# Last layer of a two-layer kernel: squares turned by TensorE, taps' end and mixed sum ahead of the last down product

## The chip, the cores and the metric

The kernel runs on one core of a Trainium2 chip. The metric is the device time of one execution in microseconds (us). The engines are TensorE (PE, with its weight loads PEld), VectorE (DVE), ScalarE (ACT), GpSimd (POOL) and SyncE (SP), which issues the DMAs.

## What is computed

Two layers over 8 sequences of 512 tokens with 128 channels. The first layer is attention times a mixture of experts; the second, which the change is in, is a gated recurrent block times a tanh feed-forward:

```python
def _L1_attn_ref(x, ...):
    h = rmsnorm(x, norm1_w)
    local = causal_depthwise_conv(h, conv_w)          # 7 taps
    decay = jnp.clip(jax.nn.sigmoid(h @ Wdecay + bdecay), 0.05, 0.95)
    gate = jax.nn.sigmoid(h @ Wgate + bgate)
    updates = gate * h
    cumdecay = jnp.exp(jnp.cumsum(jnp.log(decay), axis=1))
    weighted_updates = updates / jnp.maximum(cumdecay_shifted, 1e-07)
    state = jnp.cumsum(weighted_updates, axis=1) * cumdecay * state_scale
    mem = (h @ Wk) @ M.T @ Wmem * mem_scale
    mixed = x + jnp.concatenate([local, state, mem], axis=-1) @ Wc + bc
    h2 = rmsnorm(mixed, norm2_w)
    return mixed + jax.nn.silu(h2 @ Wg) * (h2 @ Wup) @ Wdown
...
x = x + s * g     # s from above, g = silu(tanh(xn @ weight @ aux_weight1 @ aux_weight2 + bias))
```

`rmsnorm` divides by the root of the mean square over the channels. The change concerns how `h2` gets this mean square, and when `mixed` of the next sequence is made.

## The kernel before

Every engine has a program written by hand, and semaphores tie them together; nothing but the written order and the waits sets when an instruction runs. The last layer goes over the eight sequences in steps b = 0 to 7, each with tiles of 128 channels by 512 tokens. While step b does the feed-forward of sequence b, it prepares sequence b+1 (turning, gates, decay, taps, state) and, through ACT and POOL, sequences b+2 to b+4 (normalising, gate of the first layer). Products go to eight banks of PSUM.

Names that the trace shows for tiles are those of the regions they lie in: `SPARE`, `WGE`, `W1E`, `W2E` hold the last layer's tiles. Lines of TensorE in a step: `d_conv_end` L975 and `d_state` L979 close bank 4 (taps, memory, state); `d_turn_scaled` L925, `d_ffn1` L985, `d_back` L1052 (turns the finished product of b-1 back), `d_squares` L992, `d_gates` L947 and L950, `d_roots` L998 (spreads the inverse roots), `d_turn` L933, `d_conv` L971, then four chunks c of `d_up` (L1012 gate, L1018 up) and four of `d_down` (L1044).

VectorE: `d_mixed` L1510, the radicands of sequence b+2 L1456 and L1459, `d_meansq` L1517 (mean square plus epsilon, `SSE`), `d_local` L1524 (taps 1 to 5, each adds to `LOC`), `d_add` L1572 (adds the product of b-1 to X), `d_h2_of` L1530, `d_decay` L1483, `d_cumulate` L1488, `d_floor` L1496, `d_gated` L1537 (four), `d_mean_scaled` L1476, `d_scan` L1503, `d_sum` L1568 (down product plus mixed), statistics L1445 and L1450.

GpSimd: `gate_out` L625 (waits for `d_sum`), `front` L594 and `add_x` L599 (sequence b+3), `rms` L629 (power -0.5 of `SSE`, waits for `d_meansq`, releases `d_roots`), `scales` L610, `update_gated` L615, `update` L620 (waits for the floor; the scan waits for it), `both` L634 (sequence b+4). ScalarE makes the squares of `mixed` (L1931) and copies, tanh and SiLU.

Before, the squares `SQR` are the weights of four matmuls with one column `MEAN` = 1/128, which gives the mean square of each token in one column of PSUM.

Of the kernel before, what the change touches and what calls it, by code (L numbers as in the profile page):

```python
# [26 lines left out]
P = 128  # L27
# [53 lines left out]
def build(nc, t, out):  # L81
    ctx = ExitStack()
    with ctx:
# [46 lines left out]
        MEAN = sb("MEAN", [P, 1])  # L130
# [107 lines left out]
        ST1 = small[:, 8 * TPS:14 * TPS].rearrange("p (i s) -> p i s", s=6)  # L238
        SSE, RS = (small[:, (16 + n) * TPS:(17 + n) * TPS] for n in range(2))
# [91 lines left out]
        done = sem("done")  # L331
# [14 lines left out]
        d_own = sem("d_own")  # L346
        d_xp, d_ve, d_vv, d_r1, d_hs, d_trh, d_da, d_gp, d_u1 = (
# [24 lines left out]
        def mixed(b):  # L372

            return MIXL if b == NSEQ - 1 else MIX

        def roots_bank(b):

            return 0 if b == NSEQ - 1 else 7

        def back_bank(b):  # L380

            return 1 if b == NSEQ - 2 else 5
# [122 lines left out]
        def _(pool):  # L505
# [143 lines left out]
            for b in range(NSEQ):  # L649
                if b == 0:  # L650
                    pool.wait_ge(d_sta, 1)
                    add_x(2)
                    both(3)
                elif b < NSEQ - 1:
                    gate_out(b - 1)
                    if b + 3 < NSEQ:
                        front(b + 3)
                        add_x(b + 3)
# [14 lines left out]
        def _(pe):  # L673
# [115 lines left out]
            def count():  # L789
# [4 lines left out]
                pe.wait_ge(prep, 3)  # L794
# [61 lines left out]
            pe.wait_ge(prep, 3)  # L856
# [61 lines left out]
            def d_turn_scaled(b):  # L918
                pe.wait_ge(d_hs, b + 1)
                if not (isinstance(b, int) and b == 0):  # L920
                    pe.wait_ge(d_ht, b)
                else:
                    pe.wait_ge(proj_free, 4 * NSEQ)
                for i in range(TPS):
# [62 lines left out]
            def d_squares(b):  # L987
                pe.wait_ge(d_sq, b + 1)
                if 0 < b < NSEQ - 1:
                    pe.wait_ge(d_s, b)  # L990
                for i in range(TPS):
                    mm = pe.matmul(B[roots_bank(b)][:, i:i + 1], SQR[:, i * P:(i + 1) * P], MEAN[:], start=True, stop=True)  # L992
                mm.then_inc(d_ss, 1)

            def d_roots(b):
                pe.wait_ge(d_rs, b + 1)
                for i in range(TPS):
                    mm = pe.transpose(B[roots_bank(b)][:, i * P:(i + 1) * P], RS[:, i:i + 1].broadcast_to([P, P]), ident)  # L998
# [49 lines left out]
            def d_back(b):  # L1048
                pe.wait_ge(d_of, b + 1)
                pe.wait_ge(d_sil, FC * b + FC)  # L1050
                for i in range(TPS):
                    mm = pe.transpose(B[back_bank(b)][:, i * P:(i + 1) * P], OF[:, i * P:(i + 1) * P], ident)  # L1052
                mm.then_inc(d_ot, 1)

            def d_step(b, first=False, last=False):

                if not first and not last:
                    d_conv_end(b)
                if not last:
# [20 lines left out]
                down = d_last_down if last else (lambda c: d_down(b, c))  # L1080
                down(0)
                d_up(b, 3)
                down(1)
# [13 lines left out]
            pe.wait_ge(prep, 3)  # L1097
# [7 lines left out]
            d_first_conv()  # L1105
            d_step(0, first=True)
# [8 lines left out]
        def _(dve):  # L1115
# [76 lines left out]
            def slots():  # L1192
# [5 lines left out]
                dve.wait_ge(prep, 3)  # L1198
# [365 lines left out]
            def d_sum(b):  # L1564
# [15 lines left out]
            def d_step(b, first=False, front=True):  # L1580
                if front and not first:
                    d_later_stats(b + 2)
                d_mixed(b)
# [22 lines left out]
                if b == NSEQ - 2:  # L1606
                    d_scan(b + 1)
                    d_gated(b, 3)
                    d_mixed(b + 1)
                else:  # L1610
                    d_gated(b, 3)
                    d_scan(b + 1)
                d_sum(b)

            def d_last_step(b):
# [458 lines left out]
```

## Time and profile before

| | us |
|---|---|
| median of 3 runs | 540.2 |
| lowest, highest | 539.59, 540.52 |
| profiled execution, its own time | 540.95 |
| its span, first to last instruction | 538.8 |
| PE busy | 519.0 (96%) |
| DVE busy | 397.5 (74%) |
| ACT busy | 314.6 (58%) |
| POOL busy | 223.7 (42%) |

The last layer fills the span from about 377 us on. A share of the whole span is an average over stages, so the stage is read in stretches: one for each step, from the end of the step's state product to the end of the next. The chain of waits goes backwards from the last instruction and tells which engine held the end. The timeline gives each instruction's start, its length and, in brackets, how long its engine had been idle and what ended that. [...]

### The profile page before, as it was taken

What the parts mean: (1) busy time and instruction counts of PE and PEld (TensorE: products, weight loads), DVE (VectorE), ACT (ScalarE), POOL (GpSimd) and SP (SyncE); (2) the same over time, 40 slices, a digit from 0 to 9 for tenths busy, and PEclk for the clock granted to TensorE, in tenths of its full rate; (3) what the DMA queues carried; (4) which work ended last, traced back from release to release, by engine and by line L of the source; (5) the groups of instructions that cost most, each with busy time, mean ns of one, the idle gap of its engine ahead of it and who ended that gap; (6) DMA issues with size and microseconds to landing.
All of it is one profiled execution on the core that took longest, in us unless ns stands there. A gap on an engine that the chain in (4) does not pass through costs nothing. (4 is left out here: it accounts for less than half of the span.)

```text
span 538.8 us, 12865 instructions
## 1 busy us (share of the span) xinstructions
PE 519.0 (96%) x3195; PEld 387.7 (72%) x3196; DVE 397.5 (74%) x1129; ACT 314.6 (58%) x832; POOL 223.7 (42%) x229
## 2 busy tenths in 40 slices
PE   9998898999998999999999999998999999999997
PEld 4755566666667999999999999986454545544544
DVE  6889669768885766777677767766788887788654
ACT  4733554555547656666666666667776576657512
POOL 4304453666640333333333333332667557623310
PEclk9999999999999999999999999999999999999999
DMA  9930743311126555555555555618300000000001
GB/s 283 395 115 28 229 152 127 99 60 66 40 45 52 155 131 156 132 155 138 152 137 152 141 151 141 151 47 225 94 0 21 0 20 21 19 0 21 19 7 33
DMA packets 84722, 55.37 MB, mean 103 GB/s; under 512 B 52928, under 2 KB 69600, under 8 KB 84432
## 3 DMA queue, kind: packets, MB, share of 16 engines
q1 hardware_dynamic: 80368, 46.04, 32.7%
q0 software_dynamic: 4320, 8.92, 4.6%
q8 instruction: 16, 0.26, 0.2%
q14 instruction: 18, 0.15, 0.1%
HBM read 37.62 MB, written 15.74 MB: 99 GB/s over the span
## 5 line engine op out<-in xcount | busy, mean ns | idle before, releaser
L1808 ACT ACTIVATE AR<-bank,BGT 128x128 f32<-128x128 f32 x284 | 81.2, 368 | 71.8 <-PE bank L870 69.6
L580 POOL DMA_INDIRECT rows_y<-YO,W1E x71 | 68.8, 969 | 126.5 <-DVE YO L1335 123.9
L541 POOL DMA_INDIRECT slots_x<-XR,SLOT x64 | 62.5, 977 | 52.6 <-DMA slots_x<-XR,SLOT 32.7
L1358 DVE SCALAR_TENSOR_TENSOR AR<-bank,B1T,AR 128x128 f32<-128x128 f32 x284 | 80.2, 344 | 5.1 <-ACT AR L1808 3.6
L870 PE MATMUL bank<-AR,WGE 128*128 128x128 f32 x568 | 76.7, 278 | 1.9 <-DVE AR L1341 1.7
L888 PE MATMUL bank<-W2E,AR 128*128 x568 | 75.1, 275 | 0.5 <-DVE AR L1358 0.5
L879 PE MATMUL bank<-AR,WGE 128*128 128x128 f32 x568 | 75.0, 275 | 0.0
L1724 ACT ACTIVATE AR<-bank,AR 128x512 f32<-128x512 f32 (+1 forms) x64 | 33.8, 528 | 64.2 <-DVE AR L1268 53.4
L870 PEld LDWEIGHTS bank<-AR,WGE 128*128 128x128 f32 x568 | 69.0, 192 | 2.9 <-issue 2.5
L888 PEld LDWEIGHTS bank<-W2E,AR 128*128 128x128 f32 x568 | 69.1, 192 | 0.7 <-issue 0.7
L879 PEld LDWEIGHTS bank<-AR,WGE 128*128 128x128 f32 x568 | 69.1, 192 | 0.0
L785 PE MATMUL bank<-AR 128*128 128x128 f32 x320 | 48.2, 281 | 2.8 <-ACT AR L1733 1.8
L1341 DVE STREAM_TRANSPOSE AR<-XG 128x128 f32<-128x128 f32 x71 | 22.1, 311 | 37.3 <-issue 22.3
L1268 DVE TENSOR_REDUCE AR<-bank 128x1 f32<-128x512 f32 (+1 forms) x64 | 31.1, 488 | 25.0 <-PE bank L752 19.1
L1801 ACT ACTIVATE WGE<-SPARE 128x512 f32 x71 | 45.4, 641 | 0.8 <-issue 0.5
L785 PEld LDWEIGHTS bank<-AR 128*128 128x128 f32 x320 | 40.7, 191 | 5.9 <-ACT AR L1733 4.6
L750 PE MATMUL bank<-AR 128*128 128x128 f32 (+3 forms) x128 | 45.0, 435 | 0.0
L766 PEld LDWEIGHTS bank<-CST,AR 128*128 128x128 f32 x160 | 18.9, 141 | 29.7 <-ACT AR L1724 15.9
L766 PE MATMUL bank<-CST,AR 128*128 128x128 f32 x160 | 29.1, 280 | 6.2 <-ACT AR L1724 5.8
L1948 ACT ACTIVATE W1E<-bank 128x512 f32<-128x512 f32 x32 | 19.0, 593 | 26.8 <-PE bank L1012 26.8
L1012 PE MATMUL bank<-WGE,WGT 128*128 128x512 f32 x64 | 32.7, 593 | 0.7 <-DVE X L1572 0.7
L1018 PE MATMUL bank<-WGE,WUP 128*128 128x512 f32 x64 | 32.7, 592 | 0.0
(214 smaller groups left out, 910.9 us busy)
## 6 DMA issues: line engine op xcount, KB each, us to landing
WGE<-in_wgu SPq DMA_DIRECT2D x71, 256.0 KB
XG<-slots_x SPq DMA_DIRECT2D x140, 32.0 KB
slots_x<-W1E SPq DMA_DIRECT2D x7, 585.0 KB, 10.1
X<-in_x SPq DMA_DIRECT2D x8, 256.0 KB, 5.1
SPARE<-in_wgu SPq DMA_DIRECT2D x1, 2048.0 KB
W2E<-in_w SPq DMA_DIRECT2D x1, 2048.0 KB
XR<-rows_y SPq DMA_DIRECT2D x8, 256.0 KB, 4.9
XNT<-rows_y SPq DMA_DIRECT2D x8, 256.0 KB, 5.4
```

The costliest lines, as they stand in the source:

```text
L541: pool.indirect_dma_start(out=slots_x, out_offset=bass.IndirectOffsetOnAxis(ap=SLOT[:, k, n:n + 1], axis=0), in_=XR[:, n, :], in_offset=No ...
L580: pool.indirect_dma_start(out=rows_y, out_offset=bass.IndirectOffsetOnAxis(ap=DST[:, j:j + 1], axis=0), in_=YO[q % 2][:], in_offset=None). ...
L750: pe.matmul(bank[:, 0:(i + 1) * P], QT[u][h][:, i * P:(i + 1) * P], QT[u][2][:, 0:(i + 1) * P], start=True, stop=False)
L766: mm = pe.transpose(B[4 + k % 2][:, j * P:(j + 1) * P], PR[k % 2][:, j * P:(j + 1) * P], ident)
L785: mm = pe.matmul(reg, PT[k % 2][:, j * P:(j + 1) * P], U[u][:, j, h * P:(h + 1) * P], start=(j == 0), stop=(j == i))
L870: mm = pe.matmul(B[1 + u][:, c * P:(c + 1) * P], WB[:, q, c * P:(c + 1) * P], XT[u], start=True, stop=True)
L879: mm = pe.matmul(B[3 + u][:, c * P:(c + 1) * P], WU[:, u, c * P:(c + 1) * P], XT[u], start=True, stop=True)
L888: mm = pe.matmul(B[5 + u][:, 0:P], HT[u][:, c, :], W2E[:, bass.ds(e, 1), c, :], start=(c == 0), stop=(c == FC - 1))
L1358: s = dve.scalar_tensor_tensor(out=HT[u][:, c, :], in0=B[3 + u][:, c * P:(c + 1) * P], scalar=B1T[:, bass.ds(e, 1), c], in1=ZB[u][:, c, :] ...
L1724: act.activation(PR[k % 2][:, 0:(i + 1) * P], B[2 + k % 2][:, 0:(i + 1) * P], ACT.Exp, bias=NM[:, k:k + 1], accum_out=DEN[:, k:k + 1]).the ...
L1801: act.activation(WU[:, u:u + 1, :], SPARE[:, bass.ds(e, 1), :], ACT.Copy).then_inc(c_wu, 1)
L1808: act.activation(ZB[u][:, c, :], B[1 + u][:, c * P:(c + 1) * P], ACT.Gelu, bias=BGT[:, bass.ds(e, 1), c]).then_inc(c_gelu, 1)
```

## The change

Squares. `d_squares` turns the four tiles of `SQR` into bank 0 by transposes; VectorE adds up each token's 128 columns (`tensor_reduce` into `SSQ`) and then forms `SSE` as `SSQ / 128 + eps`. `MEAN` and the ACT operation that made it go. The roots are spread in bank 7 in every step; `d_back` uses bank 1 in every step.

Order. `d_conv_end(b+1)`, `d_state(b+1)` and VectorE's `d_mixed(b+1)` stand at the end of step b, ahead of the last down product, which opens the next step of TensorE. `mixed` alternates between two tiles (`MIX`, `MIXL`). On VectorE `d_sum(b-1)` opens the step, `d_h2_of` stands ahead of `d_add`, `d_floor` ahead of `d_mean_scaled`, `d_scan` ahead of the third gated product and taps 4 and 5, and the statistics of b+3 ahead of `d_mixed(b+1)`. On GpSimd `front(b+3)` and `add_x(b+3)` stand behind `update_gated` instead of ahead of `rms`, from step 1 on. `d_turn_scaled` waits for `d_out`, `d_turn` for `d_sse`, `d_roots` for `d_s`; the gate product no longer waits for `d_out`.

```diff
 # gpsimd
                 elif b < NSEQ - 1:
                     gate_out(b - 1)
-                    if b + 3 < NSEQ:
-                        front(b + 3)
-                        add_x(b + 3)
                 rms(b)
...
                     update_gated(b + 1)
+                    if b > 0 and b + 3 < NSEQ:
+                        front(b + 3)
+                        add_x(b + 3)
                     update(b + 1)
 # tensor
             def d_squares(b):
                 pe.wait_ge(d_sq, b + 1)
-                if 0 < b < NSEQ - 1:
+                for i in range(TPS):
+                    mm = pe.transpose(B[0][:, i * P:(i + 1) * P], SQR[:, i * P:(i + 1) * P], ident)
+                mm.then_inc(d_ss, 1)
+
+            def d_roots(b):
+                pe.wait_ge(d_rs, b + 1)
+                if b > 0:
                     pe.wait_ge(d_s, b)
                 for i in range(TPS):
-                    mm = pe.matmul(B[roots_bank(b)][:, i:i + 1], SQR[:, i * P:(i + 1) * P], MEAN[:], start=True, stop=True)
-                mm.then_inc(d_ss, 1)
...
             def d_step(b, first=False, last=False):
 
-                if not first and not last:
-                    d_conv_end(b)
+                if not first:
+                    d_down(b - 1, 3)
                 if not last:
-                    d_state(b)
                     d_turn_scaled(b + 1)
                     d_ffn1(b)
+                    d_squares(b)
+                    d_gates(b + 1)
                     if not first:
                         d_back(b - 1)
-                    d_squares(b)
-                    d_gates(b + 1)
                     d_roots(b)
                     d_turn(b + 1)
                     d_conv(b + 1)
                 else:
+                    d_ffn1(b)
                     d_squares(b)
-                    d_ffn1(b)
-                    keep_warm(3, 2)
+                    keep_warm(3, 8)
                     d_back(b - 1)
...
+                else:
+                    d_down(b, 0)
+                    d_up(b, 3)
+                    d_down(b, 1)
+                    d_down(b, 2)
                     d_conv_end(b + 1)
                     d_state(b + 1)
-                down(2)
-                down(3)
 # vector
             def d_meansq(b):
                 dve.wait_ge(d_ss, b + 1)
+                dve.tensor_reduce(SSQ, B[0][:].rearrange("p (i d) -> p i d", d=P), AX.X, ALU.add).then_inc(d_ssq, 1)
+                dve.wait_ge(d_ssq, b + 1)
                 if not (isinstance(b, int) and b == 0):
                     dve.wait_ge(d_rs, b)
-                dve.tensor_scalar(SSE, B[roots_bank(b)][:, 0:TPS], RMS_EPS, None, ALU.add).then_inc(d_sse, 1)
+                dve.tensor_scalar(SSE, SSQ, 1.0 / P, RMS_EPS, ALU.mult, ALU.add).then_inc(d_sse, 1)
...
             def d_step(b, first=False, front=True):
-                if front and not first:
-                    d_later_stats(b + 2)
-                d_mixed(b)
+                if not first:
+                    d_sum(b - 1)
...
                 d_local(b + 1, 1)
+                d_h2_of(b)
                 if not first:
                     d_add(b - 1)
-                d_h2_of(b)
                 d_decay(b + 1)
                 d_cumulate(b + 1)
                 d_gated(b, 0)
+                d_floor(b + 1)
                 if front:
                     d_mean_scaled(b + 2)
-                d_floor(b + 1)
                 d_local(b + 1, 2)
                 d_gated(b, 1)
                 d_local(b + 1, 3)
+                d_scan(b + 1)
                 d_gated(b, 2)
                 d_local(b + 1, 4)
                 d_local(b + 1, 5)
...
+                d_gated(b, 3)
+                if b + 3 < NSEQ:
+                    d_later_stats(b + 3)
+                d_mixed(b + 1)
```

TensorE's rows around the border between two steps, before:

```order
L1044 MATMUL bank7<-W1E,WDN 128x512 x3
L975 MATMUL bank4<-SPARE,W3 128x512
L979 MATMUL bank4<-WGE,WST 128x512
L925 MATMUL bank1<-CST,SPARE 128x128 x4
L985 MATMUL bank6<-WGE,GF 128x512
L1052 MATMUL bank5<-CST,SPARE 128x128 x4
L992 MATMUL bank7<-MEAN,WGE 128x1 x4
L947 MATMUL bank3<-W2E,W3 128x512
L950 MATMUL bank2<-W2E,W3 128x512
L998 MATMUL bank7<-CST,SPARE 128x128 x4
```

And after (L1037 is the down product, L970 and L974 the taps' end and the state, L985 the squares, L1045 `d_back`, L993 the roots):

```order
L1037 MATMUL bank7<-W1E,WDN 128x512 x2
L970 MATMUL bank4<-SPARE,W3 128x512
L974 MATMUL bank4<-WGE,WST 128x512
L1037 MATMUL bank7<-W1E,WDN 128x512
L919 MATMUL bank1<-CST,SPARE 128x128 x4
L980 MATMUL bank6<-WGE,GF 128x512
L985 MATMUL bank0<-CST,WGE 128x128 x4
L942 MATMUL bank3<-W2E,W3 128x512
L945 MATMUL bank2<-W2E,W3 128x512
L1045 MATMUL bank1<-CST,SPARE 128x128 x4
L993 MATMUL bank7<-CST,SPARE 128x128 x4
```

The last down product moved from ahead of the taps' end to behind the state product, `d_back` behind the gates, and the squares became four 128x128 transposes.

VectorE's rows from the cumulative product to the next mixed sum in step 1, before:

```order
L1488 SCALAR_TENSOR_TENSOR W2E<-WGE,SPARE 128x512
L1537 TENSOR_TENSOR W1E<-bank6,W1E 128x512
L1476 SCALAR_TENSOR_TENSOR SPARE<-SPARE 128x8
L1496 TENSOR_SCALAR SPARE<-W2E 128x512
L1524 SCALAR_TENSOR_TENSOR SPARE<-W2E,VEC,SPARE 128x512
L1537 TENSOR_TENSOR W1E<-bank3,W1E 128x512
L1524 SCALAR_TENSOR_TENSOR SPARE<-W2E,VEC,SPARE 128x512
L1537 TENSOR_TENSOR W1E<-bank6,W1E 128x512
L1524 SCALAR_TENSOR_TENSOR SPARE<-W2E,VEC,SPARE 128x512 x2
L1537 TENSOR_TENSOR W1E<-bank3,W1E 128x512
L1503 SCALAR_TENSOR_TENSOR WGE<-WGE 128x512
L1568 TENSOR_TENSOR SPARE<-bank7,WGE 128x512
```

And after, from tap 3 (L1522) on to the reduction (L1511):

```order
L1522 SCALAR_TENSOR_TENSOR SPARE<-W2E,VEC,SPARE 128x512
L1499 SCALAR_TENSOR_TENSOR WGE<-WGE 128x512
L1535 TENSOR_TENSOR W1E<-bank6,W1E 128x512
L1522 SCALAR_TENSOR_TENSOR SPARE<-W2E,VEC,SPARE 128x512 x2
L1535 TENSOR_TENSOR W1E<-bank3,W1E 128x512
L1441 BN_STATS SPARE<-X 128x6 x4
L1506 SCALAR_TENSOR_TENSOR WGE<-bank4,VEC,WGE 128x512
L1566 TENSOR_TENSOR SPARE<-bank7,W2E 128x512
L1446 BN_AGGR SPARE<-SPARE 128x2 x4
L1452 SCALAR_TENSOR_TENSOR SPARE<-SPARE 128x4
L1455 SCALAR_TENSOR_TENSOR SPARE<-SPARE 128x4
L1511 TENSOR_REDUCE SPARE<-bank0 128x4
```

The scan (old L1503, new L1499) moved ahead of taps 4 and 5, and the sum (old L1568, new L1566) behind the mixed sum, directly ahead of aggregates and radicands.

GpSimd's rows of one step with front work, before:

```order
L625 TENSOR_TENSOR SPARE<-SPARE,WGE 128x512
L594 TENSOR_TENSOR XR<-XR,SA 128x512
L599 TENSOR_TENSOR X<-X,XR 128x512
L629 TENSOR_TENSOR SPARE<-SPARE,HALF 128x4
L610 TENSOR_TENSOR SPARE<-SPARE,HALF 128x8
L615 TENSOR_TENSOR WGE<-WGE,W2E 128x512
L620 TENSOR_TENSOR WGE<-WGE,SPARE 128x512
L634 TENSOR_TENSOR XR<-XR,XNT 128x512
```

And after:

```order
L617 TENSOR_TENSOR SPARE<-SPARE,WGE 128x512
L621 TENSOR_TENSOR SPARE<-SPARE,HALF 128x4
L602 TENSOR_TENSOR SPARE<-SPARE,HALF 128x8
L607 TENSOR_TENSOR WGE<-WGE,W2E 128x512
L586 TENSOR_TENSOR XR<-XR,SA 128x512
L591 TENSOR_TENSOR X<-X,XR 128x512
L612 TENSOR_TENSOR WGE<-WGE,SPARE 128x512
L626 TENSOR_TENSOR XR<-XR,XNT 128x512
```

`front` and `add_x` (L594 and L599, now L586 and L591) moved from between `gate_out` and `rms` to between `update_gated` and `update`.

## Rows read from the trace of the kernel before

**Rows 1.** Stretches: length, each engine's busy us (instructions), granted clock, DMA share, GB/s.

```profile
390.75:409.34 18.59, 18.19 (x58) 8.76 (x57) 16.09 (x32) 12.41 (x24) 11.83 (x9) 1.00 0.00 0
...
446.26:464.49 18.23, 18.23 (x62) 9.35 (x61) 14.96 (x29) 12.01 (x23) 10.84 (x9) 1.00 0.06 16
...
517.47:538.80 21.33, 17.74 (x69) 9.86 (x67) 9.30 (x16) 4.23 (x7) 1.40 (x1) 1.00 0.09 25
```

**Rows 2.** Chain of waits, steps 3 and 7: start us, us, what.

```profile
447.99 0.92 PE bank L992 x8
448.92 0.97 PE bank L947 x2
449.88 0.86 PE bank L950 x2
450.74 0.44 PE bank L998 x4
...
524.01 1.10 PE bank L1012 x2
```

**Rows 3.** Timeline of DVE, step 3: start, us, line, operation, [idle before <-releaser].

```profile
447.46 0.41 DVE L1456 SCALAR_TENSOR_TENSOR SPARE<-SPARE 128x4 f32<-128x4 f32 x1
...
448.95 0.16 DVE L1517 TENSOR_SCALAR SPARE<-bank 128x4 f32<-128x4 f32 x1 [0.88 <-PE bank L992]
...
451.22 0.75 DVE L1530 SCALAR_TENSOR_TENSOR WGE<-bank,VEC,WGE 128x512 f32<-128x512 f32 x1 [0.68 <-PE bank L998]
452.54 0.89 DVE L1483 SCALAR_TENSOR_TENSOR WGE<-WGE,SPARE 128x512 f32<-128x512 f32 x1 [0.57 <-ACT WGE L1877]
453.46 1.23 DVE L1488 TENSOR_TENSOR_SCAN W2E<-WGE,SPARE 128x512 f32<-128x512 f32 x1
...
455.26 0.42 DVE L1496 TENSOR_SCALAR SPARE<-W2E 128x512 f32<-128x512 f32 x1
455.59 0.74 DVE L1524 SCALAR_TENSOR_TENSOR SPARE<-W2E,VEC,SPARE 128x512 f32<-128x512 f32 x1
...
456.86 1.16 DVE L1524 SCALAR_TENSOR_TENSOR SPARE<-W2E,VEC,SPARE 128x512 f32<-128x512 f32 x1
...
462.81 0.69 DVE L1568 TENSOR_TENSOR SPARE<-bank,WGE 128x512 f32<-128x512 f32 x1 [0.52 <-PE bank L1044]
```

**Rows 4.** Timeline of POOL, step 3.

```profile
445.35 1.28 POOL L625 TENSOR_TENSOR SPARE<-SPARE,WGE 128x512 f32<-128x512 f32 x1 [4.43 <-DVE SPARE L1568]
...
446.58 1.28 POOL L594 TENSOR_TENSOR XR<-XR,SA 128x512 f32<-128x512 f32 x1
...
449.19 1.02 POOL L629 TENSOR_TENSOR SPARE<-SPARE,HALF 128x4 f32<-128x4 f32 x1
...
450.19 1.64 POOL L610 TENSOR_TENSOR SPARE<-SPARE,HALF 128x8 f32<-128x8 f32 x1
...
451.79 1.09 POOL L615 TENSOR_TENSOR WGE<-WGE,W2E 128x512 f32<-128x512 f32 x1
...
455.75 1.71 POOL L620 TENSOR_TENSOR WGE<-WGE,SPARE 128x512 f32<-128x512 f32 x1 [2.87 <-DVE SPARE L1496]
...
457.43 1.71 POOL L634 TENSOR_TENSOR XR<-XR,XNT 128x512 f32<-128x512 f32 x1
```

**Rows 5.** Timeline of DVE and of POOL in step 0.

```profile
403.01 2.83 DVE L1524 SCALAR_TENSOR_TENSOR SPARE<-W2E,VEC,SPARE 128x512 f32<-128x512 f32 x2
...
403.70 1.59 POOL L599 TENSOR_TENSOR X<-X,XR 128x512 f32<-128x512 f32 x1
```

**Rows 6.** Groups by form, last layer: line, operation, count | busy us, mean ns | idle before.

```profile
L1537 DVE TENSOR_TENSOR W1E<-bank,W1E 128x512 f32<-128x512 f32 x32 | 21.7, 679 | 5.7 <-PE bank L1018 5.5
```

**Rows 7.** Timeline of DVE in the attention stage.

```profile
366.71 0.69 DVE L1268 TENSOR_REDUCE AR<-bank 128x1 f32<-128x512 f32 x1 [1.47 <-PE bank L752]
```

**Rows 8.** Timeline of POOL and of PE in step 1.

```profile
412.54 1.46 POOL L629 TENSOR_TENSOR SPARE<-SPARE,HALF 128x4 f32<-128x4 f32 x1
...
414.06 0.65 PE L998 MATMUL bank<-CST,SPARE 128*128 128x128 f32 x4 [0.20 <-POOL SPARE L629]
```

More of the change, by code:

```diff
@@ L372, in mixed @@
         def mixed(b):
[L374 to L382, printed above, removed]
+            return MIXL if b % 2 else MIX
         def half_cols(half):
@@ L793, in count @@
                 pe.wait_ge(one_set, 1)
-                pe.wait_ge(prep, 3)
+                pe.wait_ge(prep, 2)
                 pe.matmul(B[7][:, NT * E:2 * NT * E], ONB[:], MB, start=True, stop=True)
@@ L855, in _ @@
             pe.wait_ge(w_gf, 1)
-            pe.wait_ge(prep, 3)
+            pe.wait_ge(prep, 2)
             attend(0, 0, first=True)
@@ L923, in d_turn_scaled @@
                     pe.wait_ge(proj_free, 4 * NSEQ)
+                if b > 2:
+                    pe.wait_ge(d_out, b - 2)
                 for i in range(TPS):
@@ L931, in d_turn @@
                     pe.wait_ge(d_xnt, b)
+                    pe.wait_ge(d_sse, b)
                 for i in range(TPS):
@@ L1004, in d_up @@
                     pe.wait_ge(d_h2, b + 1)
-                    if not (isinstance(b, int) and b == 0):
-                        pe.wait_ge(d_out, b)
                 elif c == 1:
@@ L1079, in d_step @@
                 d_up(b, 2)
[L1080 to L1083, printed above, removed]
                 if last:
+                    d_last_down(0)
+                    d_up(b, 3)
+                    d_last_down(1)
                     d_mixed_back()
-                if b == NSEQ - 2:
+                    d_last_down(2)
+                    d_last_down(3)
+                else:
+                    d_down(b, 0)
+                    d_up(b, 3)
+                    d_down(b, 1)
+                    d_down(b, 2)
                     d_conv_end(b + 1)
                     d_state(b + 1)
-                down(2)
-                down(3)
             pe.wait_ge(c_ht, SLOT_TILES)
@@ L1096, in _ @@
             pe.wait_ge(w_ready, 3)
-            pe.wait_ge(prep, 3)
+            pe.wait_ge(prep, 2)
             pe.wait_ge(exp_done, NS * NSEQ)
@@ L1105, in _ @@
             d_first_conv()
+            d_state(0)
             d_step(0, first=True)
@@ L1197, in slots @@
                 link(dve.tensor_scalar(TCN, REM, ULP_IS_P, None, ALU.subtract))
-                dve.wait_ge(prep, 3)
+                dve.wait_ge(prep, 2)
                 link(dve.tensor_tensor_scan(CTL, ONES, TCN, 0.0, ALU.mult, ALU.add))
@@ L1505, in d_mixed @@
             def d_mixed(b):
-                if 0 < b < NSEQ - 1:
-                    dve.wait_ge(d_s, b)
+                if b > 1:
+                    dve.wait_ge(d_s, b - 1)
                 dve.wait_ge(d_xnt, b + 1)
@@ L1529, in d_h2_of @@
                 dve.wait_ge(d_mix, b + 1)
-                dve.scalar_tensor_tensor(out=H2, in0=B[roots_bank(b)][:], scalar=VEC[:, V_N2:V_N2 + 1], in1=mixed(b), op0=ALU.mult,
+                dve.scalar_tensor_tensor(out=H2, in0=B[7][:], scalar=VEC[:, V_N2:V_N2 + 1], in1=mixed(b), op0=ALU.mult,
                                          op1=ALU.mult).then_inc(d_h2, 1)
@@ L1567, in d_sum @@
                     dve.wait_ge(d_ot, b)
-                dve.tensor_tensor(OF, B[7][:], MIX, ALU.add).then_inc(d_s, 1)
+                dve.tensor_tensor(OF, B[7][:], mixed(b), ALU.add).then_inc(d_s, 1)
             def d_add(b):
                 dve.wait_ge(d_ot, b + 1)
-                dve.tensor_tensor(X[:, tiles(b), :], X[:, tiles(b), :], B[back_bank(b)][:].rearrange("p (i d) -> p i d", d=P),
+                dve.tensor_tensor(X[:, tiles(b), :], X[:, tiles(b), :], B[1][:].rearrange("p (i d) -> p i d", d=P),
                                   ALU.add).then_inc(d_out, 1)
@@ L1605, in d_step @@
                 d_local(b + 1, 5)
[L1606 to L1613, printed above, removed]
+                d_gated(b, 3)
+                if b + 3 < NSEQ:
+                    d_later_stats(b + 3)
+                d_mixed(b + 1)
             def d_last_step(b):
+                d_sum(b - 1)
                 d_meansq(b)
@@ L1647, in _ @@
             d_scan(0)
+            d_mixed(0)
             d_step(0, first=True)
@@ L1661, in _ @@
         def _(act):
-            act.wait_ge(one_set, 1)
-            act.activation(MEAN[:], ONB[:, 0:1], ACT.Copy, scale=1.0 / P).then_inc(prep, 1)
             def normalise(b):
```

10 lines of the change are left out of this document (5 added, 5 removed).

## The prediction, made before the changed kernel was timed

> **What bounds the kernel now.** Read the stretches first [rows 1]. From 446.26 to 464.49 lies one step of the last layer: 18.23 us, in which TensorE (PE) is busy for all 18.23, VectorE (DVE) for 14.96, GpSimd (POOL) for 10.84. Then the chain of waits [rows 2]: inside the step it never leaves PE, so a step lasts as long as its matmuls. But DVE has only 3.3 us to spare, so the third thing to read is what DVE and POOL do to each other [rows 3, 4].
>
> Below, T(b) is the end of the state product of step b, the point from which VectorE can make `mixed(b)`. In the trace T(0) is 390.75, T(1) 409.34, T(3) 446.26, T(4) 464.49, and the last, T(7), 517.47 [rows 1]. Small numbers are us after T, three-digit ones times of the trace.
>
> **DVE and POOL shut each other out.** A tap (`d_local`, L1524) takes 0.74 alone, at 455.59. At 456.86 it takes 1.16: POOL's L620 runs from 455.75 to 457.46, and 457.46 + 0.56 is its end, 458.02. At 452.54 L1483 takes 0.89: POOL's L615 ends at 452.88, and 0.55 later it ends. The 128x4 operation L1456 takes 0.41 at 447.46, where one at 448.95 takes 0.16: it ends at 447.87, POOL's L594 at 447.86 [rows 3, 4]. So a DVE operation with two SBUF inputs that meets a running POOL elementwise operation starts its data only when POOL ends (0.56 more for 128x512; a scan of 1.23 alone some 1.08 more). The other way too: POOL's L634, issued at 457.43, ends at 459.14, 1.12 after the tap. Who is next, a pair shows [rows 5]: two taps in a row take 2.83, from 403.01 to 405.84, and the second ends 0.55 after POOL's L599 (403.70 + 1.59 = 405.29): between two DVE operations in a row the waiting POOL operation gets in. DVE operations with a PSUM input are not held: all 32 of L1537 have a mean of 0.68 [rows 6]. [...]
>
> [...] With the rule a step comes out at the 20.9 below, without any hold at 17.8: it speaks against the new place of POOL's work.
>
> **What the change takes away.** The squares were 4 matmuls in two passes, 0.92 in the chain, and the gate behind them was slowed to 0.97 from the usual 0.86. Turning the squares costs what another group of four transposes costs, 0.44 [rows 2]. PE work per step: 18.23 - 0.48 - 0.11 = 17.64. Everything else on PE is only in another order (18 products of 0.86, five groups of 0.44). The ACT operation at the start and its `prep` count go: one of 128x1, in a stretch that the chain doesn't reach, nothing. The waits added for `d_out`, `d_s`, `d_sse` on PE ask for work a step or several us older: nothing. The last product ahead of squares (`d_down(b-1, 3)`) hides `mixed` and the square: the squares' slot moves from 1.73 to 2.16 while both still start at T.
>
> **What it adds: the path to the roots.** DVE gets a `tensor_reduce` of PSUM 128x512. The nearest row is the attention's, 0.69 for one output column [rows 7]; 0.66 of it counts, since the next operation starts 0.03 to 0.08 ahead of an end. It can't be below 0.42, the floor L1496 on SBUF, and above I take 0.75, h2 at 451.22, which reads PSUM and SBUF [rows 3]. PE order after T: down 0.86, turn scaled 1.30, ffn1 2.16, squares 2.59, gates 4.31, back 4.75, then roots. DVE: `mixed` 0.1 to 0.85, `d_sum(b-1)` after the down product, 1.0 to 1.67 (0.69 as at 462.81), aggregates to 1.97, then the radicands at 2.0. But `d_sum` releases POOL's `gate_out`, 1.75 to 3.02 (1.28 at 445.35) [rows 4]. The radicands L1452 (old L1456) are two-SBUF-input operations: held until 3.03, the second to 3.23. Reduce 3.27 to 3.93, SSE to 4.13 (0.16, as at 448.95), POOL's power 1.02 from 4.21 to 5.23. In step 1 of before the power ended at 414.00 and the roots at 414.71, 0.71 later [rows 8]. So the roots end at 5.94, not 5.18: PE stalls 0.76, more than the 0.59 gained. Without the held radicands it would be 3.60, 4.62, 5.33: a stall of 0.14.
>
> **What it adds: the path to the taps' end.** `d_conv_end(b+1)` and the state product now stand ahead of the last down product, and on DVE the scan stands ahead of taps 4 and 5, `d_add` behind h2. More important, POOL's `front` and `add_x`, which ran at 446.58 to 449.2 while DVE waited for squares [rows 4], now run behind `update_gated`, in DVE's densest stretch. Steps 1 to 3 after roots at 5.94: h2 to 6.73 (0.75), add to 7.32 (0.68). POOL: scales to 6.85 (1.64), `update_gated` to 7.92 (1.10). Then the two alternate. Decay wants 7.24, is held, ends 8.47. `front` ends 9.60 (8.47 + 1.13). The cumulative product, issued at 8.5, is held and ends 10.69. `add_x` 11.82. First gated product (PSUM) 11.29, floor 12.10, mean scaled 12.22, tap 2 12.88, `update` 14.01, gated 13.48, tap 3 held to 14.56, `both` 15.69, scan held to 16.77, gated 17.37, then POOL is idle and taps 4 and 5 (0.75 each and 0.1 between, since the second reads what the first wrote) end at 18.89.
>
> PE would be ready for the taps' end at 16.69. A 512-column product that really waits takes 1.10 (at 524.01) instead of 0.86 and starts some 0.08 after its release (448.95 + 0.16 to POOL's 449.19): 0.32 more [rows 2 to 4]. So it runs from 19.21 to 20.07, the state product to 20.93: **a step of 20.93 instead of 18.23**, DVE-bound. Without contention tap 5 would end near 15.3 and nothing stall.
>
> **Sum.** Step 0 has no `gate_out`, but PE waits for squares (0.50 instead of 0.46 before) and POOL's power; and from 11.5 on `front(3)`, `add_x(3)`, `both(4)` fall between tap 3, the scan, taps 4 and 5, so tap 5 ends at 17.66 and T(1) is 390.75 + 19.70 = 410.45 (before 409.34). Steps 1 to 3: 3 x 20.93 to 473.24. Step 4 has no `both`: 19.85, to 493.09. Step 5 has no front work but still radicands behind `gate_out`: 18.41, to 511.50. Step 6 has neither: 17.64 + 0.14, to 529.3. Last step: roots at 5.32 after T, h2 to 6.11, the gate product from 6.19, where it was 6.54 (524.01 - 517.47) since it also waited for `d_add`. 8 warm-up products instead of 2 lie in the wait for the power. From there 14.79 to the end as before: 20.98. Span 550.3 against 538.8, +11.5. The profiled execution took 540.95, so 552.45 for it; the median of the runs is 0.75 lower: **551.7 us**.
>
> **Rivals.** (A) The forecast, DVE and POOL alternating. Its own unknowns: the scan gets the port ahead of `both` (-0.66 in three steps), the floor is not held (-0.4 a step), the radicands are not (-0.6 in five): 547 at the least, 554 with a reduce of 0.75 in eight steps and one hold of 0.5 more in three of them. (B) The change does what its words say: PE stays the bound. For it: 14.96 + 0.66 us of DVE is below 17.64. Against it: [rows 3, 4], where each two-input operation that starts under a POOL operation is held to its end. Then T(7) is 390.75 + 17.7 + 6 x 17.78 = 515.1, the end 20.98 later, 536.1, time 537.5. (C) Only the power's path gets late, because the new POOL order falls kindly: steps 1 to 5 of 18.41, step 6 of 17.78, T(7) = 518.3, end 539.3, time 540.7: no change. (D) The change doesn't turn the squares at all but only reorders: excluded, the rows of the order show bank0<-CST,WGE 128x128 x4. The slow side is A: it decides from the moment at which tap 5 ends later than 16.37 after T (16.69 - 0.32), which needs 1.1 us of held time; I count 3.5.
>
> **How the numbers follow.** A 0.80, B 0.12, C 0.08 (half of it within 0.2%, half slower). A measurement of this kernel tells about 0.2%, 1.1 us, from no change. Faster 0.12, same 0.04, slower 0.84. A alone holds 547 to 554. To leave out no more than 2 in 10 the range has to reach C: 540.5 to 554.
>
> **What would show it.** In the profile after: steps 1 to 3 near 20.9 us, PE busy near 17.6 of it; PE idle ahead of the taps' end and the third down product, released by DVE's local and gated product; the decay, cumulative product, taps 3 and the scan of those steps at 1.1 to 2.3 us instead of 0.69 to 1.23; radicands of about 1.0 us; the roots ending 1.2 after `d_back` instead of 0.44. Steps 5 and 6 near 18.4 and 17.8. It is wrong if POOL's `front` and `add_x` run beside DVE's decay and cumulative product with both at their lengths alone, or if DVE's idle time in steps 1 to 3 is more than 2 us. The granted clock is 1.00 in every stretch of before; if the new waits of PE lowered it, every product would be longer and the time above my range.

## The result, and the profile after

| | before | after |
|---|---|---|
| median of the runs, us | 539.89 (6 runs) | 553.48 (6 runs) |
| lowest, highest | 537.68, 543.36 | 552.03, 556.93 |
| profiled execution, its own time | 540.95 | 552.89 |
| its span | 538.8 | 550.7 |

The changed kernel takes 1.0247 of the time before, 95% interval 1.0215 to 1.028: slower. The forecast was 551.7 us (range 540.5 to 554), with a span of 550.3 and 552.45 for the profiled execution.

Section 1 of the page of after: busy us, share of the span, count of instructions.

```profile
PE 520.2 (94%) x3169; PEld 383.8 (70%) x3170; DVE 414.6 (75%) x1137; ACT 315.7 (57%) x831; POOL 232.2 (42%) x229
```

DVE and POOL are busy 17.1 and 8.5 us longer than before, although one small reduce per step is all that DVE has more to do and POOL has the same instructions. Where that lies is told by the stretches of after, cut like [rows 1] from state product to state product (steps 0, 2, 4, 5, 6 and the last; 1 and 3 read like 2): length, busy us of PE, weight loads, DVE, ACT, POOL, granted clock, DMA share, GB/s.

```profile
390.28:410.13 19.85, 17.23 (x52) 7.82 (x50) 17.11 (x32) 12.64 (x24) 12.57 (x8) 1.00 0.00 0
...
431.18:452.23 21.05, 18.43 (x58) 8.60 (x57) 18.38 (x30) 12.01 (x23) 12.63 (x8) 1.00 0.04 13
...
473.29:493.26 19.97, 18.43 (x57) 8.60 (x57) 17.30 (x30) 11.49 (x22) 10.94 (x7) 1.00 0.05 13
493.26:511.48 18.22, 17.86 (x57) 8.84 (x57) 15.22 (x26) 11.61 (x22) 6.75 (x5) 1.00 0.05 15
511.48:529.69 18.21, 17.85 (x57) 8.84 (x57) 13.12 (x19) 8.55 (x14) 5.52 (x4) 1.00 0.05 15
529.69:550.70 21.01, 17.90 (x69) 9.56 (x67) 10.00 (x17) 4.22 (x7) 1.39 (x1) 1.00 0.09 25
```

Where [rows 1] had a step of 18.23 with DVE busy for 14.96 and POOL for 10.84, step 2 now has 21.05, 18.38 and 12.63. PE, which had filled its step, is idle for 2.6 us of it. The excess is in the steps that still carry `front` and `add_x`; steps 5 and 6, which don't, stand at 18.2.

The chain of waits had stayed on PE [rows 2]. In step 2 of after it leaves PE behind the down product, at 432.08, and comes back to it only for the roots and then at the taps' end (start, us, what):

```profile
432.08 0.70 DVE SPARE L1566
...
432.85 1.27 POOL SPARE L617
...
435.23 1.48 POOL SPARE L621
...
436.75 0.66 PE bank L993 x4
...
437.44 0.75 DVE WGE L1528
...
438.78 1.14 DVE WGE L1479
...
444.73 1.17 DVE SPARE L1522
...
449.44 0.76 DVE SPARE L1522
...
450.25 1.12 PE bank L970 x2
```

And what PE waited for in steps 1 to 7 of after (who waits <- who releases: us in total, times, longest us):

```profile
PE bank L1037 <- DVE W1E L1535: 4.6, 4, 1.4
PE bank L993 <- POOL SPARE L621: 4.2, 7, 0.8
PE bank L970 <- DVE SPARE L1522: 1.6, 4, 0.4
```

So there are two places: the roots (L993), late in all seven, and the end of VectorE's row of taps and gated products (L970, L1037), late in four. The two timelines of step 2 show why. VectorE, T(2) = 431.18 (start, us, line, operation, [idle before <- releaser]):

```profile
433.09 1.05 DVE L1452 SCALAR_TENSOR_TENSOR SPARE<-SPARE 128x4 f32<-128x4 f32 x1
...
434.26 0.68 DVE L1511 TENSOR_REDUCE SPARE<-bank 128x4 f32<-128x512 f32 x1
434.97 0.17 DVE L1515 TENSOR_SCALAR SPARE<-SPARE 128x4 f32<-128x4 f32 x1
435.06 0.75 DVE L1522 SCALAR_TENSOR_TENSOR SPARE<-W2E,VEC,SPARE 128x512 f32<-128x512 f32 x1
437.44 0.75 DVE L1528 SCALAR_TENSOR_TENSOR WGE<-bank,VEC,WGE 128x512 f32<-128x512 f32 x1 [1.62 <-PE bank L993]
...
438.70 1.21 DVE L1479 SCALAR_TENSOR_TENSOR WGE<-WGE,SPARE 128x512 f32<-128x512 f32 x1
439.94 2.18 DVE L1484 TENSOR_TENSOR_SCAN W2E<-WGE,SPARE 128x512 f32<-128x512 f32 x1
...
442.63 0.84 DVE L1492 TENSOR_SCALAR SPARE<-W2E 128x512 f32<-128x512 f32 x1
...
444.73 1.16 DVE L1522 SCALAR_TENSOR_TENSOR SPARE<-W2E,VEC,SPARE 128x512 f32<-128x512 f32 x1
445.81 2.28 DVE L1499 TENSOR_TENSOR_SCAN WGE<-WGE 128x512 f32<-128x512 f32 x1
```

GpSimd in the same step:

```profile
432.85 1.27 POOL L617 TENSOR_TENSOR SPARE<-SPARE,WGE 128x512 f32<-128x512 f32 x1 [6.88 <-DVE SPARE L1566]
435.22 1.47 POOL L621 TENSOR_TENSOR SPARE<-SPARE,HALF 128x4 f32<-128x4 f32 x1 [1.10 <-DVE SPARE L1515]
...
439.32 1.72 POOL L586 TENSOR_TENSOR XR<-XR,SA 128x512 f32<-128x512 f32 x1
441.12 2.07 POOL L591 TENSOR_TENSOR X<-X,XR 128x512 f32<-128x512 f32 x1
```

The decay L1479 takes 1.21 (0.89 in [rows 3]), the cumulative product L1484 2.18 where [rows 3] had it at 1.23, the scan L1499 2.28, and `front` L586 takes 1.72 where it took 1.28 beside an almost idle VectorE [rows 4]; `add_x` L591 takes 2.07. They interleave: decay to 439.91, `front` to 441.04, cumulative product to 442.12, `add_x` to 443.19, the floor to 443.47.

### The profile page after: what moved, and what is told of

Read it like the earlier page. It is cut to its first block, busy times and chain, and to the rows that moved or that the text cites. A ratio compares the mean times of both kernels' runs of the same rounds, so it can differ in the third digit from the quotient of the medians.

```text
span 550.7 us, 12814 instructions
## 1 busy us (share of the span) xinstructions
PE 520.2 (94%) x3169; PEld 383.8 (70%) x3170; DVE 414.6 (75%) x1137; ACT 315.7 (57%) x831; POOL 232.2 (42%) x229
## 4 chain that ended last, share of the span: by engine, by line
PE 64%; DVE 17%; issue 10%; POOL 5%; ACT 2%; DMA 1%; POOLq 0%; DVEq 0%; SPq 0%; ACTq 0%
PE bank L862 12%; PE bank L880 11%; PE bank L871 11%; PE bank L742 5%; PE bank L777 5%; DVE SPARE L1522 3%; PE bank L721 3%; PE bank L726 3%; PE bank L758 2%; POOL SPARE L621 2%; POOL SPARE L617 1%; PE bank L1005 1%; PE bank L1037 1%; PE bank L1011 1%; PE bank L684 1%
## 5 line engine op out<-in xcount | busy, mean ns | idle before, releaser
L1037 PE MATMUL bank<-W1E,WDN 128*128 128x512 f32 x56 | 28.5, 600 | 4.6 <-DVE W1E L1535 4.6
```

## The experiments

In each the steps are read from one state product's end to the next. Three bounds compete for one step: PE's matmuls, 17.64 by the forecast's working; the roots, which in the new order those matmuls need by 5.18 after T, so that later roots add what they are late; and VectorE's row up to tap 5 and the scan. The steps are compared and not the whole times where a run was timed once: the stage began at T(0) = 391.41 in one of these runs and between 385.55 and 386.11 in the others, although nothing ahead of it differs.

**The squares alone, on the kernel before.**

```diff
-                    mm = pe.matmul(B[roots_bank(b)][:, i:i + 1], SQR[:, i * P:(i + 1) * P], MEAN[:], start=True, stop=True)
+                    mm = pe.transpose(B[roots_bank(b)][:, i * P:(i + 1) * P], SQR[:, i * P:(i + 1) * P], ident)
...
+                dve.tensor_reduce(SSQ, B[roots_bank(b)][:].rearrange("p (i d) -> p i d", d=P), AX.X, ALU.add
+                                  ).then_inc(d_ssq, 1)
+                dve.wait_ge(d_ssq, b + 1)
-                dve.tensor_scalar(SSE, B[roots_bank(b)][:, 0:TPS], RMS_EPS, None, ALU.add).then_inc(d_sse, 1)
+                dve.tensor_scalar(SSE, SSQ, 1.0 / P, RMS_EPS, ALU.mult, ALU.add).then_inc(d_sse, 1)
```

> The kernel before, with nothing changed but the squares: four transposes into the bank of the roots and a reduction on VectorE instead of the four one-column matmuls. Orders as before. My account (the roots wait for GpSimd's power, and a tap on VectorE that starts ahead of the power holds it): squares end 2.2 after T, reduction 3.0, SSE 3.2, the tap behind it holds the power to 4.7, roots end 5.4 where they ended 4.9, so steps of 18.7 instead of 18.23 and a time some 0.4 to 0.6% above before, about 543. Rival, the words of the change (PE is the bound, the squares cost less): steps of 17.6, time about 536.

Measured: 539.81 us against 537.02 of before in the same runs, ratio 1.0067 (1.0043 to 1.0092). Steps of 18.76 (step 2), roots 5.44 after T. DVE and POOL about the roots:

```profile
426.15 0.69 DVE L1516 TENSOR_REDUCE SPARE<-bank 128x4 f32<-128x512 f32 x1 [0.48 <-PE bank L993]
...
426.96 0.75 DVE L1528 SCALAR_TENSOR_TENSOR SPARE<-W2E,VEC,SPARE 128x512 f32<-128x512 f32 x1
...
427.12 1.47 POOL L630 TENSOR_TENSOR SPARE<-SPARE,HALF 128x4 f32<-128x4 f32 x1 [0.32 <-DVE SPARE L1521]
```

Turning the squares takes 0.59 of PE's work away (from the end of the product ahead of them to that of the second gate product 2.75 in [rows 2], 447.99 to 450.74, and 2.16 in step 2 of after, 433.34 to 435.50) and brings the roots 0.52 later (5.44 for 4.92). In the old order PE could have had them at 4.92 - 0.59 = 4.33, so it waits 1.11, and 17.64 + 1.11 = 18.75 gives the step of 18.76. The time is 0.7% above before, where 0.4 to 0.6% had been expected. The power takes 1.47, not 1.02; more on that below.

**The order alone, with the old squares.**

```diff
-                    mm = pe.transpose(B[0][:, i * P:(i + 1) * P], SQR[:, i * P:(i + 1) * P], ident)
+                    mm = pe.matmul(B[0][:, i:i + 1], SQR[:, i * P:(i + 1) * P], MEAN[:], start=True, stop=True)
...
-                dve.tensor_reduce(SSQ, B[0][:].rearrange("p (i d) -> p i d", d=P), AX.X, ALU.add).then_inc(d_ssq, 1)
-                dve.wait_ge(d_ssq, b + 1)
-                dve.tensor_scalar(SSE, SSQ, 1.0 / P, RMS_EPS, ALU.mult, ALU.add).then_inc(d_sse, 1)
+                dve.tensor_scalar(SSE, B[0][:, 0:TPS], RMS_EPS, None, ALU.add).then_inc(d_sse, 1)
```

> The changed kernel with the old squares (four one-column matmuls, no reduction), all the new orders kept. My account, that the new orders put GpSimd's work against VectorE's dense stretch: steps 1 to 3 of 20.6 (21.05 in the changed kernel), time about 551, 2% above before. Rival, that the reduction and the longer path to the roots make the loss: steps of 18.2 to 18.6, time at most 542.

Measured: 544.85 against 537.02, ratio 1.0148 (1.0128 to 1.0169), steps 1 to 3 of 20.34 to 20.37. The order alone carries 2.1 of the 2.8 us that a step gained; what the squares add on top of it, 21.05 - 20.35 = 0.70, is the reduce (0.68), one for one. The chain behind it has no slack in either run: power, `scales`, `update_gated`, and the decay, which is held until 0.55 behind the end of `update_gated`, all come 0.70 earlier here than in after. The expected 20.6 was 0.25 too high, and the expected 2% of the time came out as 1.5%.

**POOL's reads taken away, its time kept.** From step 1 on the three POOL operations of the later sequences only write, and the kernel leaves out what they had computed.

```diff
+        IDLE = W2E[:].rearrange("p e c d -> p (e c d)")[:, 5 * SEQ:5 * SEQ + 1390]
...
+                if b > 3:
+                    pool.memset(IDLE, 0.0).then_inc(d_xp, 1)
+                    return
                 pool.tensor_tensor(X[:, tiles, :], X[:, tiles, :], Y0[:, tiles, :], ALU.add).then_inc(d_xp, 1)
```

> The changed kernel in which, from step 1 on, GpSimd's front, add_x and both are replaced by memsets of 1390 elements into an unused place: the same engine is busy about as long (1.3 us each) in the same order, but reads nothing; the output lacks that work. My account, that VectorE's two-input operations wait for a running GpSimd operation that reads SBUF: the cumulative product 1.23 instead of 2.18, the scan 1.23 instead of 2.28, steps 1 to 3 of about 18.9 instead of 21.05. Rival, that GpSimd is merely late with update because front and add_x stand ahead of it: nothing gets shorter, steps of 21.

Measured: 540.26 against 537.02, ratio 1.007 (1.0048 to 1.0091); steps 1 to 3 of 18.66 to 18.67. DVE and POOL in step 2:

```profile
433.14 1.23 DVE L1496 TENSOR_TENSOR_SCAN W2E<-WGE,SPARE 128x512 f32<-128x512 f32 x1
...
434.86 0.48 DVE L1504 TENSOR_SCALAR SPARE<-W2E 128x512 f32<-128x512 f32 x1
...
436.60 1.16 DVE L1534 SCALAR_TENSOR_TENSOR SPARE<-W2E,VEC,SPARE 128x512 f32<-128x512 f32 x1
...
432.50 1.25 POOL L589 MEMSET W2E<- 128x1390 f32 x1
433.81 1.26 POOL L597 MEMSET W2E<- 128x1390 f32 x1
435.43 1.78 POOL L620 TENSOR_TENSOR WGE<-WGE,SPARE 128x512 f32<-128x512 f32 x1 [0.36 <-DVE SPARE L1504]
```

This is the run that decides between "POOL's turn is in the way" and "POOL's access to SBUF is in the way". POOL is as long busy at the same places (2 x 1.25), but the cumulative product beside it takes 1.23, as alone; tap 3, beside an `update` that still reads, takes 1.16. The operation was changed together with its reads (a memset for a `tensor_tensor`), so the run tells a writing operation from a reading one, and no more. The step falls by 2.4 us, and what is left of its excess is the roots: 17.64 + (6.21 - 5.18) = 18.67.

**POOL's work moved behind `both`, alone.**

```diff
-                    if b > 0 and b + 3 < NSEQ:
-                        front(b + 3)
-                        add_x(b + 3)
                     update(b + 1)
-                if b == 0:
-                    front(3)
-                    add_x(3)
                 if b + 4 < NSEQ:
                     both(b + 4)
+                if b + 3 < NSEQ:
+                    pool.wait_ge(d_sta, b + 2)
+                    front(b + 3)
+                    add_x(b + 3)
```

VectorE's statistics of these tiles go with it, to behind `d_sum` of the next step.

> The changed kernel with GpSimd's front and add_x of b+3 behind both and behind the scan, statistics of b+2 behind the sum; radicands and scan stay where the change put them. The simple reading (front and add_x between update_gated and update are the fault) gives steps of 18.7 in steps 1 to 3. My account gives no gain at all, about 21: since the scan stands ahead of taps 4 and 5, the two operations that it releases now hold these taps.

Measured: 549.75 in one run (beside 535.43 of before), steps of 21.21. No gain. Timelines of step 2, DVE then POOL:

```profile
440.79 2.28 DVE L1497 TENSOR_TENSOR_SCAN WGE<-WGE 128x512 f32<-128x512 f32 x1
...
443.58 3.06 DVE L1520 SCALAR_TENSOR_TENSOR SPARE<-W2E,VEC,SPARE 128x512 f32<-128x512 f32 x2
...
443.15 1.27 POOL L586 TENSOR_TENSOR XR<-XR,SA 128x512 f32<-128x512 f32 x1 [1.16 <-DVE WGE L1497]
444.50 1.59 POOL L591 TENSOR_TENSOR X<-X,XR 128x512 f32<-128x512 f32 x1
```

The scan's end releases `front`, and taps 4 and 5, which stand behind the scan, meet it and `add_x`: the two taps take 3.06 instead of the 1.59 of after. The cumulative product and the floor are not held any more (1.23 and 0.42 here), but what they give back, 0.95 + 0.42, the taps take, 1.47. The first radicand isn't held either, since the statistics (0.86) now stand ahead of it; the reduce ends no earlier for that, at 3.84 for 3.76, and the roots at 6.31 for 6.22.

**The scan moved behind taps 4 and 5, alone.**

```diff
-                d_scan(b + 1)
                 d_gated(b, 2)
                 d_local(b + 1, 4)
                 d_local(b + 1, 5)
+                d_scan(b + 1)
                 d_gated(b, 3)
```

> The changed kernel with the scan behind taps 4 and 5 and nothing else; front and add_x stay between update_gated and update. My account: taps end near 17.2 after T, the scan near 18.3, steps 1 to 3 of 19.5. If the place of the scan were indifferent: 21.05.

Measured: 542.4 in one run beside 535.43, steps 1 to 3 of 19.58 to 19.60: 1.47 us a step less than after. The scan is not held any more and no longer stands ahead of the taps that PE needs first. The step now ends with it: the scan's end at 18.41, 0.08 and a waiting product of 1.10 make 19.59.

**Both moves.** The two edits above together.

> As the one before, and the scan behind taps 4 and 5 as well; radicands stay ahead of the reduction. My account: taps end before PE needs them, only the roots' path stalls: steps of 18.7 in steps 1 to 3, roots 6.2 after T. If the place of the scan doesn't matter: the same as the kernel before this one.

Measured: 538.36 in one run, steps of 18.75 and 18.76. The pair is worth 2.29 us a step, where one alone gives 1.47 and the other -0.16. With the scan behind the taps, `front`, which it releases, starts beside the last gated product, which reads PSUM: 1.26 at 439.49 beside 0.67 at 439.33, both as long as alone. What remains of the excess is the roots, at 6.31: 17.64 + (6.31 - 5.18) = 18.77.

**The mean square ahead of the radicands, alone, on after.**

```diff
+                d_meansq(b)
                 if front:
                     d_aggregate(b + 2)
                     d_radicands(b + 2)
-                d_meansq(b)
```

> The changed kernel with one thing moved on VectorE: aggregates and radicands of b+2 behind the SSE instead of ahead of the reduction. They then are not held by gate_out, and they stand between the SSE and the tap, so the tap no longer holds GpSimd's power. Roots should end 5.4 after T instead of 6.2. If the path to the roots were what makes steps 1 to 3 long, they would fall by 0.8 to 20.2; my account, in which the stretch from the decay to the taps' end sets the end, gives 20.5.

Measured: 550.38 in one run, roots at 5.33, steps of 20.29 to 20.31. The roots come 0.89 earlier, as the first radicand, held for 1.05 by `gate_out`, is out of their way; the step falls by 0.75. Both expected figures (20.2 and 20.5) are near. The rows of step 2 (T at 431.24, POOL then DVE) tell which bound it is:

```profile
435.84 1.78 POOL L602 TENSOR_TENSOR SPARE<-SPARE,HALF 128x8 f32<-128x8 f32 x1
437.59 1.09 POOL L607 TENSOR_TENSOR WGE<-WGE,W2E 128x512 f32<-128x512 f32 x1
...
437.87 1.35 DVE L1479 SCALAR_TENSOR_TENSOR WGE<-WGE,SPARE 128x512 f32<-128x512 f32 x1
```

`update_gated` (L607) ends at 7.44 after T instead of 8.18, and the decay (L1479), held by it, at 7.98 instead of 8.73: 0.75 earlier, like the step. The rest of the roots' 0.89 is lost in `scales` (L602), 1.78 for 1.63. So VectorE's row is the bound; roots at 5.33 alone would allow a step of 17.79.

**All three mends.** Both moves, and the mean square ahead of aggregates and radicands; the statistics of b+2 stay ahead of it.

> The changed kernel with three orders mended: GpSimd's front and add_x of b+3 behind both and behind the scan (so they run while VectorE finishes the step and makes mixed), statistics, aggregates and radicands of b+2 behind the sum and the SSE, the scan behind taps 4 and 5. If the port is the cause: cumulative product 1.23, no radicand ahead of the reduction, steps 1 to 3 of 17.7 to 18.3 and a time of 536 to 540. What is open: whether GpSimd's power holds the radicands that now stand beside it. Rival (VectorE simply has too much work): steps stay above 20.

Measured: 535.2 against 537.02, ratio 0.9966 (0.994 to 0.9993), a gain of 0.3%. The time is below the expected 536 to 540, as before, too, took 537.02 here and not 540. The cumulative product takes 1.23 in step 2, as expected. That a port is behind it is my reading: no run shows a port, only how long operations take beside others. Stretch of step 2, as above:

```profile
422.73:440.61 17.88, 17.86 (x57) 8.85 (x57) 15.69 (x30) 12.01 (x23) 11.11 (x9) 1.00 0.05 15
```

PE is busy for 17.86 of 17.88: it bounds again, but for 0.24 us of waiting for the roots (5.42 for 5.18), which the drawn lengths of the matmuls cover. DVE's 15.69 is 2.7 us less than in after for the same operations. Timelines about the roots and the scan, DVE then POOL:

```profile
426.67 0.16 DVE L1450 SCALAR_TENSOR_TENSOR SPARE<-SPARE 128x4 f32<-128x4 f32 x1
...
426.95 0.75 DVE L1520 SCALAR_TENSOR_TENSOR SPARE<-W2E,VEC,SPARE 128x512 f32<-128x512 f32 x1
...
437.85 1.22 DVE L1497 TENSOR_TENSOR_SCAN WGE<-WGE 128x512 f32<-128x512 f32 x1
...
426.43 1.02 POOL L621 TENSOR_TENSOR SPARE<-SPARE,HALF 128x4 f32<-128x4 f32 x1 [0.75 <-DVE SPARE L1513]
...
439.15 1.27 POOL L586 TENSOR_TENSOR XR<-XR,SA 128x512 f32<-128x512 f32 x1 [2.62 <-DVE WGE L1497]
440.49 1.27 POOL L591 TENSOR_TENSOR X<-X,XR 128x512 f32<-128x512 f32 x1
```

Step 6 alone stayed at 18.22, its roots at 5.76. It has no radicands, so tap 1 follows `SSE` at once and starts ahead of the power.

**The same, with tap 1 behind h2 in step 6.**

```diff
-                d_local(b + 1, 1)
+                if front:
+                    d_local(b + 1, 1)
                 d_h2_of(b)
+                if not front:
+                    d_local(b + 1, 1)
```

> The three mended orders of f3_all_three, and in step 6, where no radicands stand between the SSE and the tap, the tap behind h2. In f3_all_three step 6 took 18.22 and its roots ended 5.76 after T, against 17.88 and 5.42 in the steps before. If the tap that holds GpSimd's power is the cause, step 6 falls to 17.9 and the rest stays: time 0.4% below before. If it isn't, step 6 stays at 18.2.

Measured: 537.47 against 540.35, ratio 0.9941 (0.9916 to 0.9967). Step 6 is 17.77 and its roots end at 5.32: 17.64 + 0.14. POOL's power there:

```profile
501.96 1.01 POOL L621 TENSOR_TENSOR SPARE<-SPARE,HALF 128x4 f32<-128x4 f32 x1 [0.66 <-DVE SPARE L1513]
```

This version is faster than before by 0.6%, and than after by more. Its stage, from T(0) to the end of the span, takes 145.79 where before takes 148.05: 2.26 us, or 0.4%, the expected figure; where the rest of the 0.6% lies is not shown. It keeps the whole change and gives it other places for POOL's `front` and `add_x`, the scan, the mean square and one tap.

## Why the prediction was right, and where its steps were not

Step by step, forecast and measured:

| | forecast | measured |
|---|---|---|
| step 0 | 19.70 | 19.85 |
| steps 1 to 3 | 20.93 each | 21.05, 21.05, 21.06 |
| step 4 | 19.85 | 19.97 |
| step 5 | 18.41 | 18.22 |
| step 6 | 17.78 | 18.21 |
| last step, T(7) to the end | 20.98 | 21.01 |
| roots after T, steps 1 to 3 | 5.94 | 6.22 |
| tap 5's end after T, steps 1 to 3 | 18.89 | 19.02 |

**DVE and POOL in turn.** The rule read from [rows 3 to 5] held in the new place: the waiting side gets in between two operations of the other, as `front` with its end at 441.04 between those of the decay (439.91) and the cumulative product (442.12). In steps 1 to 3 the operations of DVE and POOL from h2 to tap 5 came in the forecast order, each ending 0.12 to 0.29 later than forecast, since the power had ended 0.28 late. The run with write-only POOL operations agrees with its being the reads that count (a cumulative product of 1.23 for 2.18).

The sum and the range also have the floor held, to 12.10 after T, 0.28 behind `add_x`. No row of before shows a floor that meets a POOL operation; in after it took 0.84 at 442.63 for its 0.42 alone, to 0.28 behind `add_x`. The range has 0.66 for who "gets the port" first, scan or `both`. No run shows a port; in step 2 of after `both` ended at 447.01 and the scan at 448.09, as in the forecast's order.

**The radicands.** Forecast as held to 3.03 after T, then the reduce to 3.93. Measured 1.05 for the first (to 2.96) and the reduce to 3.76. The aside "without the held radicands 5.33" for the roots is what the run with the mean square first measured. The hold is only half of it, though: with both moves the radicand isn't held, and the roots are as late (6.31), as the statistics stand there instead. What counts is how much VectorE does ahead of the reduce.

**The term that was mis-sized: the power.** The step said "POOL's power 1.02 from 4.21 to 5.23". It took 1.47, to 5.51. The reason is in the rows that I cited: [rows 8] shows a power of 1.46 in step 1 of before, and I took only its end from it. The condition can be read within one kernel. In step 2 of after tap 1 starts at 435.06, 0.16 ahead of the power, which takes 1.47. In step 5 it is the other way round (DVE, then POOL):

```profile
497.49 0.75 DVE L1522 SCALAR_TENSOR_TENSOR SPARE<-W2E,VEC,SPARE 128x512 f32<-128x512 f32 x1 [0.27 <-issue]
...
497.30 1.02 POOL L621 TENSOR_TENSOR SPARE<-SPARE,HALF 128x4 f32<-128x4 f32 x1 [1.10 <-DVE SPARE L1515]
```

So the term is +0.45 wherever tap 1 comes first: step 6 (18.21 for 17.78) is this term alone, and moving tap 1 there gave 17.77. In the last step, which has no tap, VectorE's own last gate operation (`d_last_gate_out`) starts 0.17 ahead of the power, which takes 1.39 there, as it had taken 1.40 in before. In steps 1 to 3 the reduce, 0.17 early, paid back part of it; in step 5 it didn't arise and the forecast was 0.19 too high. That was luck and not foreseen: tap 1 of step 5 comes 0.35 later than in the other steps in every run with the reduce, and the profile names no wait for it.

**The sum.** The steps' errors (0.15, 3 x 0.12, 0.12, -0.19, 0.43, 0.03) make 0.9; the stage began 0.47 earlier (T(0) at 390.28 for 390.75). The span came out at 550.7 for 550.3. So close a hit has luck in it: what was forecast too low makes 1.1, and step 5 and the earlier start take 0.66 of it back. The medians are 13.6 us apart, the spans 11.9; runs of after reach from 552.03 to 556.93, and what spreads them was not followed up.

**Signs that were badly chosen.** "DVE idle for more than 2 us" was to speak against the forecast. DVE was idle 21.05 - 18.38 = 2.67, of that 1.62 ahead of h2, waiting for roots that wait for POOL, and 0.79 ahead of `mixed`. Some 1.1 of the former was already in my own row (SSE to 4.13 and a tap of 0.75 behind it, h2 from 5.98), so a bound of 2 us left hardly any room for the forecast itself. "PE busy near 17.6" read 18.43: the two products that waited are drawn with 1.12 each instead of 0.86, and even step 5, without them, reads 17.86.

**The rivals.** That PE stays the bound (B) fell: it is what the mended kernel does, 17.88 a step for the 17.78 of B, and what after does not. C, only the roots late, is what the write-only run shows, 18.66. Its price for steps 1 to 5 was 18.41; the power makes the difference, less the early reduce.

What carries the slowdown is thus shown piece by piece for a step of 21.05: 2.29 for the places of POOL's work (with its statistics) and the scan, 0.88 more for the order about the mean square, which leaves 17.88, 17.64 for PE and 0.24 for roots at 5.42 instead of 5.18. These shares hold in this sequence only: alone, the three moves gave -0.16, 1.47 and 0.75.

## What to carry to other kernels

Work taken from the engine that bounds is only worth what the chain that feeds it leaves: here 0.59 us of matmuls went, and the path over reduce and power took more than that back until its order was mended. Where VectorE is nearly full, as here with 14.96 of 18.23 us before, place GpSimd's elementwise work by what VectorE does beside it (products from PSUM, whose 0.66 to 0.69 us stayed here, or nothing). Where 128x512 operations of both with two SBUF inputs met in step 2 of after, VectorE's lost up to 1.1 us (the scan, 2.28 for 1.21) and GpSimd's up to 0.8 (`add_x`, 2.07 for 1.28). Try moves that release each other together: the late place of POOL's work was worth nothing alone and 0.8 us a step once the scan that releases it had moved as well.

## What the runs showed of the hardware that I had not expected

**GpSimd's power can be held by VectorE, and held VectorE in none of the rows here.** In the run with all three mends a radicand (0.16 at 426.67) and tap 1 (0.75 at 426.95) take what they take alone, beside a power of 1.02 that began at 426.43. A tap that started 0.16 ahead of the power holds it to 1.47, one 0.12 ahead (the order alone, step 2) to 1.50, and in each such case the power ends 0.86 to 0.88 behind VectorE's operation; one that started 0.01 ahead of the power of [rows 4] does not, as in this row of VectorE in step 3 of before:

```profile
449.18 0.76 DVE L1524 SCALAR_TENSOR_TENSOR SPARE<-W2E,VEC,SPARE 128x512 f32<-128x512 f32 x1
```

GpSimd's 128x512 operations did hold a tap that started behind them: in step 3 of before 1.16 at 456.86 under L620, for 0.74 alone [rows 3, 4]. The power, of 128x4, did not; the runs don't show why.

**A write-only GpSimd operation holds the floor.** With the write-only operation from 433.81 to 435.07 the floor L1504 took 0.48 for 0.42 and ended at 435.34. It had little left to meet, but its end stands 0.27 behind that of the write-only operation, as it stood 0.28 behind `add_x` in after. The cumulative product beside such operations kept its 1.23. Why the one is held by a writing operation and the other not, the runs don't show.
